# Two cross attentions and two feed-forward blocks on one core: the inverse softmax sums of the second attention spread by DMA instead of a matmul

## The chip, the cores and the metric

The kernel runs on one core of a Trainium2 chip. A core has five engines that run their own instruction streams and wait for each other through semaphores: PE (matrix products into PSUM), DVE and ACT (elementwise work on SBUF and PSUM), POOL (elementwise work, slower) and SP (here only the issuer of DMAs). Sixteen DMA engines move data between DRAM and SBUF. The metric is the device time of one execution in microseconds; of repeated runs the median is taken.

## The reference, cut to what matters

The input x is 8 batches (B) of 112 rows (S) of 512 features (D); a context has 375 tokens per batch. Four blocks follow each other, each added to x:

```
x = x + L0_xattn(layernorm(x), ctx)          # scores, softmax, readout
x = x + L0_ffn(layernorm(x))                 # ternary weights, 1408 hidden
x = x + L1_xattn(layernorm(x), ctx)          # 16 heads of 32, the block of the change
x = x + L1_ffn(layernorm(x))                 # integer weights, 1408 hidden
```

In the third block, for each head, with `Wq, Wk, Wv, Wo` and biases:

```
probs = softmax(clip(q k^T / sqrt(32), -50, 50))      # over 375 tokens
ctx   = probs v                                        # 112 x 32 for each of 16 heads
delta = layernorm(clip(residual_scale, 0, 0.3) * (ctx Wo^T + bo)) * gamma + beta
```

The kernel takes the exponentials without dividing them, sums `e v` and `e` over the tokens on PE, and multiplies the context by the inverse of the sum afterwards. The sum belongs to a head and a row; the context has 32 features for a head. So each inverse has to reach 32 partitions. The change is about that step.

## The kernel before, in words

All work is on one core, with the order of every engine's instructions written by hand in one function per engine; only what the semaphores ask is waited for. The tokens of the context are padded to 384, three chunks of 128 (TC = 3). The 896 rows of x (N) are seven tiles of 128 (TILES = 7) outside the attentions, eight batches of 112 inside.

Up to about 255 us the first attention, the first feed-forward block and the keys and values of the second attention are computed; keys and values are spilled to DRAM and fetched again batch by batch by SP (`kst`, `vst`). From 255 to 353 us the loop over the eight batches `b` of the second attention runs. The 16 heads are four groups `g` of four (G = 4), and m = 4b + g numbers the groups. A head group's context lies on 128 partitions as 4 heads x 32 features, so the context of a batch is `ctxt`, 128 partitions x (4 groups x 112 rows). For each m:

- PE `scores(m)`: 12 matmuls (L1527) into PSUM, run two groups ahead of their use.
- ACT `exps(m)`: three exponentials of 128 x 448 (L1253) into `e[g]`.
- DVE `clip(m)`: a clamp of 128 x 1344 in place (L1946).
- PE `values(b, g)`: `e v` into one PSUM bank (L1544) and `e` times the constant `z_pick` into another (L1548), which puts the sum of head `hh` of group `g` on partition 32 hh + g. In batches 0 to 3 the sums of groups 0 and 1 are first added over the token chunks by POOL (`fold`, L1025 and L1027) and picked at the end of the batch (L1556).

After the fourth group: ACT `sums_copy(b)` copies the undivided context from PSUM to `ctxt` (L1259, counts `u_copied`); DVE `invert(b)` takes the reciprocal of the sums to `rz`, 128 x 112 (L1952, counts `z_inv`); PE `spread(b)` multiplies `rz` with the constant matrix `z_spread`, four fp32 matmuls of 112 columns (L1564, counts `z_ready`), which puts inverse g of head hh on its 32 partitions in the freed sums' bank; DVE `normalize(b)` multiplies `ctxt` by that bank (L1958, counts `ctxt_scaled`); POOL `value_bias(b)` adds the values' bias (L637, counts `ctxt_ready`). The banks for context and sums alternate between (6, 7) and (4, 5) for the first batches (`D_UZ`) and are (4, 5) from batch 3 on, because banks 6 and 7 then serve the output projection; `values(b, 0)` waits until the batch before in the same banks is normalised (`UZ_BEFORE`).

Three batches behind, tile t of the output projection follows: ACT `context_high` and DVE `context_low` split the context into two halves (L653, L686), PE `project(t)` multiplies by the split `wo_p` (L673; the split itself is made in batches 2 and 3 by ACT L1283 and DVE L2001), DVE `delta_variance`, POOL `delta_inverse`, DVE `x3_statistics`, POOL `x3_inverse`, DVE `x3_shift` do the layer norms, ACT `x3_normalized`, PE `normalized_turn` (L681), ACT `turned_high` and DVE `turned_low` give the transposed input `xt` of the last block.

The order inside batch b before the change is: on PE `project(b-4)`, `spread(b-1)`, `normalized_turn(b-5)`, then scores and values of the four groups; on DVE `invert(b-1)`, second clamp, `context_low`, `normalize(b-1)`, `delta_variance`, `turned_low`, third clamp, `x3_statistics`, fourth clamp, `x3_shift`, in batch 3 the split of wo, the next batch's first clamp; on ACT `x3_normalized`, `sums_copy(b-1)`, `context_high`, `turned_high`, four groups of exponentials; on POOL `fold`, `value_bias(b-1)`, `delta_inverse`, `fold`, `x3_inverse`, integer conversion of weights. SP's queue fetches keys, values and weights.

From 353 us on the last block runs: `inner_sums(n)` are the gate and up products of one chunk of 128 hidden features (L1597), with ACT `silu_gate` (L1293) and DVE `inner_hidden` (`hf`, L2012) behind them. The first seven are interleaved with the last tiles of the projection (`project(5)`, `project(6)`), with `x3_turn` (L1606) and the late conversions of weights on ACT (`late_integers`, L1306). The down products (L1647) close the kernel.

## Time and profile before

| | |
|---|---|
| device time, median of 3 runs | 472.7 us (471.65 to 473.21) |
| the profiled execution's own time | 472.69 us |
| its span, first to last instruction | 471.0 us |
| mean granted clock of PE | 0.993 of full speed |
| busy: PE, PE weight loads | 443.2 us, 279.1 us |
| busy: DVE, ACT, POOL | 316.1, 244.7, 111.0 us |
| DMA | 82.7 MB in 59183 packets, nearly all on SP's queue |

A row of the profile gives a line of the code, the engine, the operation, its output and inputs with shapes, and times in us (ns where it says so). Busy time says how long an engine worked, not whether anything depended on it. The chain of waits, followed back from the end, tells what did. A window of the trace gives all engines' busy time in a stretch; PEclk in it is the granted clock as a share of 2.4 GHz. SPq is the queue of DMA instructions of SP; the duration of a row there is the issuing of the DMA, not its transfer, for which the time to landing is given.

### The profile page before, as it was taken

How to read it: one execution, taken by the hardware profiler on the slowest of the kernel's cores; microseconds unless marked ns; L12 is line 12 of the kernel's file. 1: busy time of each engine (PE TensorE's matmuls, PEld its weight loads, DVE VectorE, ACT ScalarE, POOL GpSimd, SP SyncE). 2: the span in 40 equal slices, each digit the busy share in tenths (PEclk: the TensorE clock that was granted, in tenths of full speed). 3: DMA queues.
4: the chain of work that ended last, by engine and by line, in shares of the span. 5: the costliest groups of instructions: out<-in, count | busy, mean ns of one | idle time of the engine just before them, and what ended most of it. 6: DMA issues, size and time to landing. Idle time of an engine off the chain costs nothing.

```text
span 471.0 us, 9958 instructions
## 1 busy us (share of the span) xinstructions
PE 443.2 (94%) x3838; PEld 279.1 (59%) x3847; DVE 316.1 (67%) x573; ACT 244.7 (52%) x370; POOL 111.0 (24%) x126
## 2 busy tenths in 40 slices
PE   8999899999899899999998888899999999999997
PEld 5556565655355345454555667577775565556996
DVE  4995596679867877765755455888867985555111
ACT  4755744764666356464847668477744682221000
POOL 2220400025024000001084364644422251000000
PEclk9999999999999999999999899899999999999999
DMA  8998988934795145333497998766242370000111
GB/s 268 328 376 310 372 292 262 330 93 146 219 295 139 53 109 160 78 91 82 111 306 197 272 316 312 266 214 225 85 135 90 90 221 26 0 0 0 48 51 58
DMA packets 59183, 82.73 MB, mean 176 GB/s; under 512 B 20100, under 2 KB 43652, under 8 KB 57988
## 3 DMA queue, kind: packets, MB, share of 16 engines
q1 hardware_dynamic: 59136, 82.14, 55.2%
q8 instruction: 29, 0.48, 0.4%
q14 instruction: 16, 0.11, 0.1%
q10 hardware_dynamic: 2, 0.01, 0.0%
HBM read 58.76 MB, written 14.42 MB: 155 GB/s over the span
## 4 chain that ended last, share of the span: by engine, by line
PE 68%; DVE 12%; SPq 7%; DMA 4%; issue 4%; ACT 2%; POOL 2%; ACTq 0%; DVEq 0%; POOLq 0%
PE psum L1597 13%; PE psum L208 8%; PE psum L206 8%; PE psum L1647 8%; PE psum L1430 6%; PE psum L673 4%; PE psum L1544 3%; PE psum L1439 3%; PE psum L1497 3%; DMA kst<-k_scratch 2%; SPq L237 2%; PE psum L1373 2%; PE psum L1527 2%; PE psum L1548 2%; DMA w_stage<-in_w 2%
## 5 line engine op out<-in xcount | busy, mean ns | idle before, releaser
L208 PE MATMUL psum<-wv_p,kv_p 128*128 128x512 f16 x288 | 66.1, 379 | 0.5 <-DVE khl L228 0.5
L206 PE MATMUL psum<-kv_p,wk_p 128*128 128x376 f16 x384 | 66.0, 322 | 0.3 <-DVE khl L228 0.3
L1253 ACT ACTIVATE e<-psum,mask_bias 128x448 f32<-128x448 f32 x96 | 53.6, 635 | 20.6 <-PE psum L1527 16.1
L206 PEld LDWEIGHTS psum<-kv_p,wk_p 128*128 128x128 f16 x384 | 37.5, 98 | 24.6 <-issue 0.6
L208 PEld LDWEIGHTS psum<-wv_p,kv_p 128*128 128x128 f16 x288 | 28.0, 98 | 32.8 <-issue 1.0
L1946 DVE TENSOR_SCALAR e<-e 128x1344 f32<-128x1344 f32 x32 | 32.3, 1010 | 11.5 <-ACT e L1253 11.5
L1544 PE MATMUL psum<-e,vst 128*32 128x112 f32 x768 | 34.9, 266 | 3.9 <-issue 3.3
L1597 PE MATMUL psum<-xt,wg_b 128*128 128x448 f16 x176 | 36.9, 352 | 0.3 <-issue 0.3
L1597 PE MATMUL psum<-xt,wu_b 128*128 128x448 f16 x176 | 36.9, 352 | 0.0
L1647 PE MATMUL psum<-h_p,wd_r 128*128 x176 | 36.0, 366 | 0.0
L1647 PEld LDWEIGHTS psum<-h_p,wd_r 128*128 128x128 f32 x176 | 33.1, 188 | 2.7
L355 POOL TENSOR_SCALAR w_stage<-w_stage,w_stat 128x2816 f32<-128x2816 f32 x6 | 17.1, 2851 | 71.9 <-DVE w_stat L350 71.8
L1293 ACT ACTIVATE gated<-psum,gs 128x448 f32<-128x448 f32 x22 | 13.9, 631 | 38.7 <-PE psum L1597 33.5
L1527 PE MATMUL psum<-qst,kst 128*128 128x112 f16 x384 | 24.9, 215 | 3.6 <-issue 3.2
L2012 DVE SCALAR_TENSOR_TENSOR hf<-psum,sgu,gated 128x448 f32<-128x448 f32 x22 | 15.0, 682 | 19.5 <-ACT gated L1293 19.3
L1597 PEld LDWEIGHTS psum<-xt,wu_b 128*128 (+1 forms) x176 | 17.2, 98 | 16.1
L1597 PEld LDWEIGHTS psum<-xt,wg_b 128*128 (+1 forms) x176 | 17.1, 98 | 15.6 <-issue 0.5
L222 ACT ACTIVATE vsp<-psum 128x512 f32<-128x512 f32 x24 | 14.1, 589 | 23.4 <-PE psum L208 23.4
L1527 PEld LDWEIGHTS psum<-qst,kst 128*128 128x128 f16 x384 | 20.2, 98 | 8.9 <-issue 6.2
L218 ACT ACTIVATE khl<-psum,bqk 128x376 f16<-128x376 f32 x32 | 18.1, 568 | 13.8 <-PE psum L206 13.7
L1544 PEld LDWEIGHTS psum<-e,vst 128*32 128x32 f32 x768 | 19.9, 111 | 7.9 <-issue 4.6
L2064 DVE SCALAR_TENSOR_TENSOR res<-psum,sdn,x3t 128x448 f32 x8 | 5.5, 684 | 28.5 <-PE psum L1647 28.5
(197 smaller groups left out, 853.9 us busy)
## 6 DMA issues: line engine op xcount, KB each, us to landing
kst<-k_scratch SPq DMA_DIRECT2D x32, 384.0 KB, 6.3
kv_raw<-in_ctx_feat SPq DMA_DIRECT2D x12, 768.0 KB, 6.3
w_stage<-in_w SPq DMA_DIRECT2D x6, 1408.0 KB, 8.7
cn<-in_ctx_tok SPq DMA_DIRECT2D x8, 768.0 KB, 9.6
k_scratch<-khl SPq DMA_DIRECT2D x128, 48.0 KB, 2.0
v_scratch<-vsp SPq DMA_DIRECT2D x24, 256.0 KB, 2.8
vst<-v_scratch SPq DMA_DIRECT2D x8, 768.0 KB, 4.6
qst<-qhl SPq DMA_DIRECT2D x32, 112.0 KB, 5.2
```

Source lines behind the costliest of these rows:

```text
L206: mm = pe.matmul(psum[:, kv_bank(p), 0:TQ], wk_p[:, u, k, n * P:(n + 1) * P], src[:, v, k, 0:TQ], **ends)
L208: mm = pe.matmul(psum[:, kv_bank(p), :], src[:, u, k, n * P:(n + 1) * P], wv_p[:, v, k, :], **ends)
L218: act.activation(khl[n][:, 0, 0:TQ], psum[:, kv_bank(p), 0:TQ], ACT.Identity, bias=bqk[:, 1, n:n + 1]).then_inc(kv_hi, 1)
L355: pool.tensor_scalar(w_stage[:, w_half_of[half]], w_stage[:, w_half_of[half]], w_stat[:, 4 * n + 2:4 * n + 3], ROUND, ALU.mult, ALU.add).t ...
L673: mm = pe.matmul(psum[:, E_O, :], ctxt_p[t % 2][:, u, k, :], wo_p[:, v, k, :], start=(k, u, v) == (0, 0, 0), stop=(k, u, v) == (KC - 1, *P ...
L1253: act.activation(e[g][:, c, :], psum[:, D_S + (TC * g + c) % 4, 0:4 * S], ACT.Exp, bias=mask_bias[:, b, c:c + 1], scale=1.0 / (WS * QS)).t ...
L1430: mm = pe.matmul(psum[:, B_GU + 2 * ((q + c) % 2) + n, 0:hi - lo], xqt[q][:, k, :], w[:, k, lo:hi], start=k == 0, stop=k == KC - 1)
L1527: mm = pe.matmul(psum[:, D_S + (TC * g + c) % 4, hh * S:(hh + 1) * S], kst[b % 2][:, g, hh, c * P:(c + 1) * P], qst[b // 4][:, hh, g, b % ...
L1544: mm = pe.matmul(psum[32 * hh:32 * hh + 32, D_UZ[b][0], g * S:(g + 1) * S], vst[b % 2][:, c, (4 * g + hh) * HD:(4 * g + hh + 1) * HD], e[g ...
L1597: mm = pe.matmul(psum[:, F_GU + 2 * q + m, 0:HALF], w[:, k, bass.ts(j, P)], xt[:, u, k, a * HALF:(a + 1) * HALF], start=(k, u) == (0, 0), ...
L1647: mm = pe.matmul(psum[:, F_D + m, 0:HALF], wd_r[:, j, m * P:(m + 1) * P], h_p[:, a, u, j, :], start=(j, u) == (0, 0), stop=(j, u) == (JC - ...
L1946: dve.tensor_scalar(e[g][:], e[g][:], EXP_LOW, EXP_HIGH, ALU.max, ALU.min).then_inc(e_ready, 1)
```

## The change

The constant `z_spread` and PE's `spread` go. ACT gets `inverse_store(b)`, a DMA of `rz` (128 x 112 floats) to one of two DRAM buffers `z_scratch`, and `inverse_load(b)`, four DMAs that each read four rows of it (one head's four groups, 448 floats in a row) and write them to the 32 partitions of that head in `zr`. `zr` has four places in SBUF, in regions that are free at the time. In batch b the store of b - 1 is issued after the exponentials m = 4b + 2 and the loads after m = 4b + 4; the store waits for the reciprocal, the loads for the store's landing. `normalize` reads `zr` from SBUF.

Around it: `normalize(b-1)` moves from the second clamp to behind the fourth clamp and `x3_shift`; POOL's `value_bias(b-1)` moves behind both folds, `delta_inverse` and `x3_inverse`; `values` and the last block wait for `u_copied` and `z_inv` in place of `ctxt_scaled`; after the loop the loads of batch 7 stand behind the first silu and `late_integers(4)`, `normalize(7)` behind `x3_statistics(4)`, and `context_high(6)`, `context_low(6)`, `delta_variance(6)` and `project(6)` move back.

```diff
-        z_spread = at("z_spread", [P, G, 4, HD], F32, 190720 + 1024)
...
+        zr = [at(f"zr{q}", [P, G, S], F32, where) for q, where in enumerate((172288, 174080, 36352, 38144))]
...
+            return zr[(2 if b >= 3 else 0) + b % 2]
...
+        z_scratch = nc.dram_tensor("z_scratch", (2, P, S), F32).ap()
...
# project
-            pe.wait_ge(ctxt_scaled, 3)
+            pe.wait_ge(u_copied, 3)
# normalized_turn
+            pe.wait_ge(z_inv, 3)
# POOL, before the loop
-            pool.memset(z_spread[:], 0.0).then_inc(ones_set, 1)
-            pool.wait_ge(ones_set, 3)
+            pool.wait_ge(ones_set, 2)
...
-            pool.affine_select(out=z_spread[:], in_=z_spread[:], compare_op=ALU.not_equal, fill=1.0, base=0,
-                               pattern=[[-1, G], [-HD, 4], [0, HD]], channel_multiplier=1).then_inc(ones_set, 1)
# POOL, the loop
                 if FOLDED[b]:
                     fold(b, 0)
-                if b:
-                    value_bias(pool, b - 1)
                 if b >= 4:
                     delta_inverse(pool, b - 4)
                 if FOLDED[b]:
                     fold(b, 1)
                 if b >= 4:
                     x3_inverse(pool, b - 4)
+                if b:
+                    value_bias(pool, b - 1)
...
+            delta_inverse(pool, 4)
             value_bias(pool, B - 1)
-            for t in range(4, TILES):
+            x3_inverse(pool, 4)
+            for t in range(5, TILES):
# ACT
+            def inverse_store(b):
+                act.wait_ge(z_inv, b + 1)
+                after(act, z_ready, 64 * (b - 1))
+                act.dma_start(z_scratch[b % 2], rz[:]).then_inc(z_stored, 16)
+            def inverse_load(b):
+                act.wait_ge(z_stored, 16 * (b + 1))
+                after(act, ctxt_scaled, b - 1)
+                if b == 3:
+                    act.wait_ge(wo_lo, 1)
+                for hh in range(4):
+                    act.dma_start(zr_of(b)[HD * hh:HD * hh + HD].rearrange("p g s -> p (g s)"),
+                                  z_scratch[b % 2, HD * hh:HD * hh + G].rearrange("(o g) s -> o (g s)", o=1)
+                                  .to_broadcast([HD, G * S])).then_inc(z_ready, 16)
...
                     if m < G * B:
                         exps(m)
+                    if b and g == 0:
+                        inverse_store(b - 1)
+                    if b and g == 2:
+                        inverse_load(b - 1)
...
             sums_copy(B - 1)
+            inverse_store(B - 1)
             context_high(act, 5)
             turned_high(act, 3)
...
             silu_gate(0, 0, 0, 0)
             late_integers(4)
+            inverse_load(B - 1)
             silu_gate(1, 1, 0, 1)
-            context_high(act, 6)
             x3_normalized(act, 4)
             late_integers(5)
             silu_gate(2, 0, 0, 2)
+            context_high(act, 6)
# PE
-                    after(pe, ctxt_scaled, UZ_BEFORE[b] + 1 if UZ_BEFORE[b] is not None else 0)
+                    if UZ_BEFORE[b] is not None:
+                        pe.wait_ge(u_copied, UZ_BEFORE[b] + 1)
+                        pe.wait_ge(z_inv, UZ_BEFORE[b] + 1)
...
-                    spread(b - 1)
...
-                    if g == 0 and 1 <= b < 4:
-                        spread(b - 1)
...
-            spread(B - 1)
...
             x3_turn(1)
+            inner_sums(3, 1, 0, 3)
             project(pe, 6)
-            inner_sums(3, 1, 0, 3)
# DVE
-                after(dve, ctxt_scaled, b)
+                after(dve, z_stored, 16 * b)
                 dve.reciprocal(rz[:], psum[:, D_UZ[b][1], 0:S]).then_inc(z_inv, 1)
...
-                dve.wait_ge(z_ready, b + 1)
+                dve.wait_ge(z_ready, 64 * (b + 1))
                 dve.wait_ge(u_copied, b + 1)
                 u = ctxt[:, :, b * S:(b + 1) * S]
-                dve.tensor_tensor(u, u, psum[:, D_UZ[b][1], 0:G * S].rearrange("p (g s) -> p g s", g=G),
-                                  ALU.mult).then_inc(ctxt_scaled, 1)
+                dve.tensor_tensor(u, u, zr_of(b)[:], ALU.mult).then_inc(ctxt_scaled, 1)
...
-                if b:
-                    normalize(b - 1)
                 if b >= 4:
                     delta_variance(dve, b - 4)
...
                 if b >= 4:
                     x3_shift(dve, b - 4)
+                if b:
+                    normalize(b - 1)
...
             turned_low(dve, 3)
-            normalize(B - 1)
...
             x3_statistics(dve, 4)
+            normalize(B - 1)
             inner_step(1, 1, 0, 1)
-            context_low(dve, 6)
             x3_shift(dve, 4)
             delta_variance(dve, 5)
             inner_step(2, 0, 0, 2)
             x3_statistics(dve, 5)
-            delta_variance(dve, 6)
+            context_low(dve, 6)
             x3_shift(dve, 5)
             inner_step(3, 1, 0, 3)
+            delta_variance(dve, 6)
```

## Rows read from the trace of the kernel before

**Rows 1.** The page, busy time, share of the span and instructions of each engine.

```profile
PE 443.2 (94%) x3838; PEld 279.1 (59%) x3847; DVE 316.1 (67%) x573; ACT 244.7 (52%) x370; POOL 111.0 (24%) x126
```

**Rows 2.** Windows: batch 3, batch 5, project(0); columns in the first line.

```profile
core 0: us, PE busy (x) PEld busy (x) DVE busy (x) ACT busy (x) POOL busy (x), PEclk, DMA share, GB/s
290.40:301.40 11.00, 8.45 (x217) 6.92 (x215) 10.92 (x8) 6.36 (x12) 9.54 (x6) 1.00 0.78 267
314.70:327.00 12.30, 12.15 (x270) 9.59 (x264) 10.46 (x19) 9.33 (x18) 5.16 (x8) 1.00 0.68 236
301.40:305.40 4.00, 4.00 (x16) 1.46 (x13) 2.51 (x4) 2.11 (x5) 1.17 (x2) 0.59 0.69 210
```

**Rows 3.** The chain of waits from 250 to 400 us, shares by line.

```profile
by line: PE psum L1597 19.3%; PE psum L673 12.6%; PE psum L1544 9.9%; DMA kst<-k_scratch 7.1%; PE psum L1527 6.5%; PE psum L1548 6.4%; issue 5.9%; PE psum L1564 3.9%; POOL zs L1027 3.1%; DVE e L1946 2.2%; ACT e L1253 2.2%; POOL zs L1025 1.9
```

**Rows 4.** Lines 1564, 1952, 1958, 1259: duration ns min/median/max, first and last start, forms.

```profile
L1564 PE MATMUL psum<-rz,z_spread x64: 259/275/515, 268.5 to 354.5; 128*128 128x112 f32 x64
...
L1952 DVE RECIPROCAL rz<-psum x8: 839/856/858, 265.4 to 352.7; 128x112 f32<-128x112 f32 x8
...
L1958 DVE TENSOR_TENSOR ctxt<-ctxt,psum x8: 607/620/622, 270.6 to 354.9; 128x448 f32<-128x448 f32 x8
...
L1259 ACT ACTIVATE ctxt<-psum x8: 543/545/551, 265.4 to 352.7; 128x448 f32<-128x448 f32 x8
```

**Rows 5.** The chain of waits in batch 5: start us, us, what.

```profile
314.81 2.70 PE psum L673 x12
317.50 0.89 PE psum L1564 x8
```

**Rows 6.** Timeline of batch 5, scores and exponentials: start us, us, engine, line.

```profile
320.63 0.77 PE L1527 MATMUL psum<-qst,kst 128*128 128x112 f16 x12
...
322.61 0.76 PE L1527 MATMUL psum<-qst,kst 128*128 128x112 f16 x12
...
323.08 1.68 ACT L1253 ACTIVATE e<-psum,mask_bias 128x448 f32<-128x448 f32 x3 [0.30 <-PE psum L1527]
```

**Rows 7.** SP's DMA instructions: issue in ns (min/median/max); landing in us of k_scratch.

```profile
L237 SPq DMA_DIRECT2D k_scratch<-khl x128: 302/427/3856, 25.6 to 232.0; - x128
...
DMA to landing us min/median/max: 1.5/2.0/10.3
...
L263 SPq DMA_DIRECT2D vst<-v_scratch x8: 325/332/597, 254.1 to 327.1; - x8
...
L560 SPq DMA_DIRECT2D qst<-qhl x32: 549/606/1784, 242.6 to 268.9; - x32
```

**Rows 8.** DMA issues, KB each, median us to landing: 262 to 300, 300 to 360 us.

```profile
kst<-k_scratch SPq DMA_DIRECT2D x15, 384.0 KB, 7.8
...
kst<-k_scratch SPq DMA_DIRECT2D x8, 384.0 KB, 5.2
```

**Rows 9.** Timeline of batch 3 and the start of batch 4.

```profile
293.52 3.25 ACT L1253 ACTIVATE e<-psum,mask_bias 128x448 f32<-128x448 f32 x6 [0.54 <-PE psum L1527]
...
294.46 1.48 POOL L637 TENSOR_TENSOR ctxt<-ctxt,bqk 128x448 f32<-128x448 f32 x1 [1.16 <-DVE ctxt L1958]
...
296.58 3.22 DVE L2001 SCALAR_TENSOR_TENSOR wk_p<-wk_raw,wk_p 128x2048 f16<-128x2048 f32 x1
...
300.84 0.59 PE L1556 MATMUL psum<-zs,z_pick 128*32 128x112 f32 x16 [2.29 <-POOL zs L1027]
...
301.37 4.45 PE L673 MATMUL psum<-wk_p,ctxt_p 128*128 128x512 f16 x12
```

**Rows 10.** Timeline of the first steps of the last block.

```profile
360.74 0.71 ACT L1306 ACTIVATE wu_b<-gu_int,zero_point 128x512 bf16<-128x512 int32 x1
...
363.87 0.67 DVE L2012 SCALAR_TENSOR_TENSOR hf<-psum,sgu,gated 128x448 f32<-128x448 f32 x1
...
367.58 2.75 PE L673 MATMUL psum<-wk_p,ctxt_p 128*128 128x512 f16 x12
...
372.49 0.18 DVE L710 BATCH_NORM_AGGREGATE ln_mv<-ln_stat 128x2 f32<-128x6 f32 x1
...
373.20 0.60 PE L681 MATMUL psum<-ident,xn_e 128*128 128x128 f32 x4
```

More of the change, by code:

```diff
@@ L564, in build, with zr_of @@
         rz = at("rz", [P, S], F32, 78080)
+        zr = [at(f"zr{q}", [P, G, S], F32, where) for q, where in enumerate((172288, 174080, 36352, 38144))]
+        def zr_of(b):
+            return zr[(2 if b >= 3 else 0) + b % 2]
+        z_scratch = nc.dram_tensor("z_scratch", (2, P, S), F32).ap()
+        z_stored = sem("z_stored")
         zs = [at(f"zs{g}", [P, 4 * S], F32, where) for g, where in enumerate((194304, 194304 + 1792))]
@@ L1007, in _ @@
             pool.memset(z_pick[:, :, G:HD], 1.0).then_inc(ones_set, 1)
-            pool.memset(z_spread[:], 0.0).then_inc(ones_set, 1)
-            pool.wait_ge(ones_set, 3)
+            pool.wait_ge(ones_set, 2)
             pool.affine_select(out=z_pick[:, :, 0:G], in_=z_pick[:, :, 0:G], compare_op=ALU.not_equal, fill=1.0, base=0,
                                pattern=[[1, G], [-1, G]], channel_multiplier=0).then_inc(ones_set, 1)
-            pool.affine_select(out=z_spread[:], in_=z_spread[:], compare_op=ALU.not_equal, fill=1.0, base=0,
-                               pattern=[[-1, G], [-HD, 4], [0, HD]], channel_multiplier=1).then_inc(ones_set, 1)
-            pool.wait_ge(ones_set, 5)
+            pool.wait_ge(ones_set, 3)
             pool.affine_select(out=z_pick_last[:], in_=z_pick[:], compare_op=ALU.is_ge, fill=0.0, base=T - 1 - 2 * P,
@@ L1537, in values @@
                     if b < 2:
-                        pe.wait_ge(ones_set, 6)
+                        pe.wait_ge(ones_set, 4)
                         pe.wait_ge(q_lo, G + 2 * (b + 1))
-                    after(pe, ctxt_scaled, UZ_BEFORE[b] + 1 if UZ_BEFORE[b] is not None else 0)
+                    if UZ_BEFORE[b] is not None:
+                        pe.wait_ge(u_copied, UZ_BEFORE[b] + 1)
+                        pe.wait_ge(z_inv, UZ_BEFORE[b] + 1)
                 for c in range(TC):
@@ L1558, in values @@
                 mm.then_inc(pv_sum, 1)
-            def spread(b):
-                pe.wait_ge(z_inv, b + 1)
-                for g in range(G):
-                    mm = pe.matmul(psum[:, D_UZ[b][1], g * S:(g + 1) * S], z_spread[:, g].rearrange("p h d -> p (h d)"), rz[:],
-                                   start=True, stop=True)
-                mm.then_inc(z_ready, 1)
             query(1, 0)
@@ L1613, in _ @@
             project(pe, 5)
-            pe.wait_ge(ctxt_scaled, B)
+            pe.wait_ge(u_copied, B)
+            pe.wait_ge(z_inv, B)
             x3_turn(0)
```

## The prediction

> **What bounds the kernel now.** I read the page first: PE is busy 94% of the span and no other engine over 67% [rows 1]. Then the windows, one for each batch of the second attention: in batch 5 PE is busy for 12.15 of 12.30 us, DVE for 10.46 and ACT for 9.33; in batch 3 PE has 8.45 us of work in 11.0 us and DVE has 10.92 [rows 2]. So PE sets the end in the later batches, with DVE 2 us behind it, and in batch 3 something else does. The chain of waits from 250 to 400 us says how much the removed matmuls hold: L1564 has 3.9% of 150 us, 5.9 us, and POOL's two sums of the folded batches 5.0% [rows 3]. That is all that the change can win directly on PE.
>
> **What is removed.** Eight spreads of 8 matmul records each [rows 4]; one takes 0.89 us on the chain in a late batch [rows 5]. POOL's two initialising steps go too; they lie beside PE's queries, where nothing waits for POOL: 0.
>
> **What is added.** For each batch ACT issues one store (128 x 112 floats, 57 KB) and four loads (57 KB each), 40 DMAs. ACT has issued none in this stretch, so their price on its queue is bounded by SP's: the 49 KB spills took 302 ns at least and 427 in the median, the plain loads of vst 332, the query stack 606 [rows 7]. The shapes are plain rows like vst's, so I take 0.33 us: a store 0.33, four loads 1.3. The first issue can lie beside the last exponential's 0.56 us (1.68 for three [rows 6]), so four loads delay ACT by 0.8. Bounds: 0 (all beside exponentials already dispatched) and 4 x 0.606 - 0.5 = 1.9. Landing: the 49 KB spills, also to DRAM, land 1.5 us after issue at least and 2.0 in the median [rows 7]; counted from the end of the issue I take 1.6, bounds 1.2 and 3.0. In the crowded stretch of batches 1 to 3, where kst takes 7.8 us against 5.2 later [rows 8], I scale that by 1.5 to 2.4.
>
> On the landing the Trainium skill speaks against the change: "DMA: Bandwidth & Descriptors", section "Anatomy of one DMA", has a fixed cost of about 2.0 us for each DMA, most of it the wait for the target memory's receipt, DRAM the slowest. The spills' 1.5 us is below it. By that figure, an estimate, the sum below would come about 1 us higher.
>
> SP's queue keeps its DMAs and their order; POOL issues none. On the 16 engines that all share, only the first store (57 KB) runs ahead of the keys of batch 2, the one load that PE waits for; it is a seventh of one 384 KB key load, and I count 0, with 1 us as the other bound.
>
> **What waits now.** The product with the inverse sums is moved behind the fourth clamp of its batch on DVE, and the load is issued by ACT only after the exponentials m = 4b + 4. So DVE, which gets there one group of exponentials earlier, stands until the landing. Queued behind are the next batch's first clamp, its reciprocal and, in batch 3, the split of wo (L2001). ACT's store in turn waits for that reciprocal. I price this in three places.
>
> Batch 3: in the trace ACT ends exponentials 15 and 16 at 293.52 + 3.25 = 296.8 and DVE starts the split of wo at 296.58 [rows 9]. After the change ACT carries six more issues in batches 2 and 3 (2.0 us, of which I hide 0.5 in its gaps): 298.3. Loads 0.8, landing 2.4, product 0.62 [rows 4], split 3.22 [rows 9]: 305.3. Project(0) needs it, and starts now at 301.4 [rows 9]. The cost is +3.9. The gain of the change is inside it: value_bias (1.48 us) no longer stands between POOL's two sums [rows 9], so PE's 2.29 us wait for POOL goes, but wo is late next. Project(0) takes 4.4 us now against 2.70 in batch 5 [rows 5, 9]: after PE's idle time the granted clock is at its lower level, 1.2 GHz, for most of it (0.59 in the window [rows 2], 1.00 in batch 5). It would be so again. 0.
>
> Batches 4 to 7: a loop of two batches. From a landing on, DVE does its whole batch until the fourth clamp, 10.5 us [rows 2] and some 0.5 of handovers: 11.0. Then PE: last values 1.3, project 2.7, transposes 0.6 [rows 10], two groups of scores and values at 1.98 each, the next scores 0.47 until the exponentials start and 1.68 for these [rows 6]: 10.75. Then loads 0.8, landing 1.6. Together 24.15, or 12.1 a batch, against 12.2 now. The 0.89 us that PE saves is thus used up by DVE's wait: -0.1 in each of three periods, -0.3.
>
> The end: the first inner sums need turned_low(3), and ACT's store, waiting for the reciprocal, now stands in front of context_high and turned_high. Context_high starts now behind the copy of the sums (0.55 [rows 4]); after the change behind reciprocal and store, 0.86 + 0.33 and some 0.1 of handovers: 1.3, so +0.8. Then the last loads stand behind ACT's silu and integers, which end at 361.4 [rows 10]: 362.2, landed 363.8, product until 364.4, so that hf of step 1 starts 0.5 later than 363.87 [rows 10]. Context_low(6) is moved behind x3_statistics(5), which ends at 372.67 [rows 10]. With 0.5 added and its own 0.7 moved out and in again it ends at 373.2, and with the 0.8 at 374.0. Project(6), now at 367.58 [rows 10], can only start then. PE has inner sums 3 beforehand and idles from 371.4, 2.6 us. The trace's row for such a gap (2.29 us) is followed by a project at the lower clock [rows 2, 9], so I take 4.4 us, not 2.75: 378.4 against 373.2 [rows 10], +5.2, of which about 1.0 comes back because DVE is then ahead of the later tiles. Cost with the 0.8: +4.2 (bounds +1.2 and +7).
>
> **Sum.** 3.9 - 0.3 + 4.2 = +7.8 us. The profiled execution took 472.69 us (span 471.0 and 1.7 around it), which is the median of the runs shown, 472.7. So 480.5. The other edits (values waiting for u_copied and z_inv in place of ctxt_scaled) cost nothing while the reciprocal comes early; it now sits behind the landing, the product and a clamp (0.62 + 1.0 + 0.84 = 2.5 us after the landing). PE comes to these values 1.3 + 2.7 + 0.6 + 0.7 = 5.3 us after the fourth clamp. So project and transposes cover it while DVE's wait for the landing stays under 2.8 us; each us more would be a us of PE.
>
> **Rivals.**
> ACT's issues are hidden and the landing is short (faster). The place is the four loads after each second pair of exponentials. It decides from the point where load issue and landing together stay under about 1.5 us. With 0 and 1.2 us the loop is (21.75 + 1.2) / 2 = 11.5, close to PE's own 12.2 - 0.9 = 11.3, so batches 4 to 7 gain 4 x 0.9 = 3.6; batch 3 then costs 0.7 (296.3 + 2.0 + 0.62 + 3.22 = 302.1) and the end 1.2: -1.7, 471.0, and down to 468 if project(6) finds cover. For it: ACT is idle for 3 of 12.3 us [rows 2]. Against it: SP's issues are nowhere under 0.3 us [rows 7], and DVE still waits for exponentials that PE produces in order. Chance 0.17.
>
> The Trainium skill is on this rival's side: the same page, section "Issuing engines are not separate DMA queues", calls the issuing time usually small relative to the DMA itself. In the rows 0.33 stands against 1.5 to 2.0, which is not small here, since five stand in one batch.
>
> Both prices at their upper end (much slower): issue 0.606, landing 3.0, because stores and loads run among 384 KB key loads. Batch 3: 299.9 + 1.9 + 3.0 + 0.62 + 3.22 = 308.6, +7.2. Loop (21.75 + 1.9 + 3.0) / 2 = 13.3, +3.4 in three periods. End +6.7. Sum +17.3, 490.0. For it: kst's 7.8 us in these stretches [rows 8]; against it: the spills' median of 2.0. Chance 0.15.
>
> It cancels (no change): the saved 0.89 us a batch pays for a shorter wait in front of wo and a tail that hides project(6); 472.7 within 1.4 us. It needs every wait at about its half. Chance 0.12.
>
> My forecast has 0.56. A measurement of this kernel can tell about 0.3%, 1.4 us. Faster 0.17, same 0.12, slower 0.56 + 0.15 = 0.71. The likeliest case alone reaches from 475 to 487. The range over all is 471 to 488, with half of the fast rival below and two thirds of the slow one above.
>
> **What would show it.** Right: DVE's product waits 2 to 5 us for the DMA in batches 1 to 3 and 0 to 2 us later; ACT shows five issues a batch of about 0.33 us; wo's split starts near 302; project(0) starts 3 to 5 us later than 301.4; batches 4 to 7 keep a period near 12.1; PE idles before project(6). Wrong: issues under 0.1 us or beside the exponentials, DVE not waiting for zr, periods of 11.4, or a split of wo that ends before PE wants it. If the keys of batch 2 land 2 us or more later, the traffic was what I missed.

## The result, and the profile after

The changed kernel takes 497.8 us (median of 4 runs, 496.3 to 498.9) against 473.0 beside it: a ratio of 1.0525 [1.0483, 1.0567], 25 us slower. The direction was right; the size was three times the predicted 7.8 us and lies outside the range of 471 to 488. Two of the traces used below, of POOL's order alone and of the changed last block alone, are of executions in a slower state (478.4 and 480.6 us against medians of 473.7 and 474.4), so they are used only to show which wait and which clock stands where.

The page after: busy time of the engines, and ACT's DMA queue. PE has 3.8 us more on its busy time than in [rows 1] although 64 matmul records are gone, because more of its work ran at the lower clock (mean 0.964 of full speed against 0.993). PE's share fell from 94% to 90%: the loss is waiting.

```profile
PE 447.0 (90%) x3774; PEld 277.7 (56%) x3783; DVE 316.1 (64%) x573; ACT 245.0 (49%) x370; POOL 114.5 (23%) x124
...
q10 hardware_dynamic: 2690, 2.31, 1.8%
```

The lines of the product (L1979), the store (L1273) and the loads (L1282): duration in ns, then what they waited for and how long they took to land. They stand for [rows 4] and [rows 7].

```profile
L1979 DVE TENSOR_TENSOR ctxt<-ctxt,zr x8: 607/626/627, 285.0 to 384.5; 128x448 f32<-128x448 f32 x8
its engine sat idle before it (us, times) until:
  DMA zr<-z_scratch: 32.9, 7
...
L1273 ACTq DMA_DIRECT2D z_scratch<-rz x8: 343/344/391, 269.2 to 371.6; - x8
...
DMA to landing us min/median/max: 1.6/2.0/8.9
...
L1282 ACTq DMA_DIRECT2D zr<-z_scratch x32: 308/445/1347, 278.1 to 380.4; - x32
...
DMA to landing us min/median/max: 1.8/2.9/7.3
```

DVE stood 32.9 us in front of seven products. By batch, issue to landing: the stores of batches 0 to 7 took 8.9, 6.2, 1.6, 3.6, 2.2, 1.6, 1.6, 1.7 us, and the longest of the four loads 5.6, 5.4, 2.9, 3.0, 7.3, 2.7, 4.9, 2.0. The two worst stores are the first two.

The timeline of batches 1 to 4, without the rows between (start us, us, engine, line; in brackets the idle time before it and its releaser):

```profile
269.15 0.39 ACTq L1273 DMA_DIRECT2D z_scratch<-rz  x1
...
275.54 1.69 ACT L1260 ACTIVATE e<-psum,mask_bias 128x448 f32<-128x448 f32 x3 [3.13 <-PE psum L1557]
...
278.08 1.74 ACTq L1282 DMA_DIRECT2D zr<-z_scratch  x4
...
285.01 0.63 DVE L1979 TENSOR_TENSOR ctxt<-ctxt,zr 128x448 f32<-128x448 f32 x1 [11.71 <-DMA zr<-z_scratch]
...
286.32 0.85 DVE L1973 RECIPROCAL rz<-psum 128x112 f32<-128x112 f32 x1
...
286.46 1.35 PE L1576 MATMUL psum<-e,vst 128*32 128x112 f32 x24 [4.75 <-DVE e L1967]
...
287.20 0.35 ACTq L1273 DMA_DIRECT2D z_scratch<-rz  x1
...
290.70 1.69 ACT L1260 ACTIVATE e<-psum,mask_bias 128x448 f32<-128x448 f32 x3 [0.62 <-PE psum L1557]
...
293.44 2.52 ACTq L1282 DMA_DIRECT2D zr<-z_scratch  x4
...
296.08 1.68 ACT L1260 ACTIVATE e<-psum,mask_bias 128x448 f32<-128x448 f32 x3 [3.70 <-issue]
...
300.96 0.63 DVE L1979 TENSOR_TENSOR ctxt<-ctxt,zr 128x448 f32<-128x448 f32 x1 [9.63 <-DMA zr<-z_scratch]
...
302.41 1.35 PE L1576 MATMUL psum<-e,vst 128*32 128x112 f32 x24 [4.75 <-DVE e L1967]
...
303.18 0.63 ACT L660 ACTIVATE ctxt_p<-ctxt 128x512 f16<-128x512 f32 x1 [3.18 <-POOL ctxt L644]
...
308.31 0.64 ACT L1260 ACTIVATE e<-psum,mask_bias 128x448 f32<-128x448 f32 x1
...
311.86 0.62 DVE L1979 TENSOR_TENSOR ctxt<-ctxt,zr 128x448 f32<-128x448 f32 x1 [3.02 <-DMA zr<-z_scratch]
...
312.40 2.29 DVE L2021 SCALAR_TENSOR_TENSOR wk_p<-wk_raw,wk_p 128x2048 f16<-128x2048 f32 x1
...
314.79 5.28 PE L680 MATMUL psum<-wk_p,ctxt_p 128*128 128x512 f16 x12 [3.60 <-issue]
```

Read it as a ring. The store goes at 269.15 and lands at 278.05; ACT, standing on that, issues the loads at 278.08; the last lands at 285.0 and DVE multiplies. Behind the product on DVE's queue are the clamp that PE's values want (PE idle 4.75 us) and the next reciprocal, which the next store wants. So the next round starts 18 us after this one, and the same happens again: store 287.20, loads 293.44, product 300.96, PE idle 4.75 us.

The rows also say which part of the ring is long. ACT ends the exponentials in front of the first loads at 275.54 + 1.69 = 277.23, so the store's 8.9 us delay the loads by only 0.85 us; the four loads themselves, issue and landing, fill 6.9 of DVE's 11.71 us. In the second round it is 1.0 us for the store and 7.5 for the loads, of DVE's 9.63. There ACT sits idle for 3.70 us with exponentials queued behind it: 1.0 of it for the store's landing, 2.5 for issuing the four loads. Later it stands 3.18 us in front of context_high(0) for POOL's value_bias. The split of wo, which I expected near 302, starts at 312.40, and project(0) at 314.79 instead of 301.37 [rows 9].

The windows of batches 1, 2, 3 and 6 (the same columns as [rows 2]):

```profile
266.00:281.50 15.50, 10.83 (x220) 8.92 (x219) 3.68 (x4) 7.15 (x13) 5.69 (x4) 0.78 1.04 307
281.50:294.90 13.40, 8.55 (x205) 7.03 (x201) 5.83 (x6) 5.51 (x11) 7.67 (x5) 0.87 0.82 284
294.90:311.00 16.10, 9.19 (x204) 7.19 (x204) 7.85 (x7) 9.95 (x17) 8.00 (x5) 0.79 0.64 206
...
341.20:357.10 15.90, 12.75 (x264) 9.91 (x256) 10.29 (x18) 8.16 (x16) 5.84 (x6) 0.89 0.48 144
```

The same for batches 1 and 2 in the kernel before:

```profile
265.30:279.00 13.70, 10.22 (x223) 8.67 (x221) 5.10 (x7) 7.31 (x14) 7.03 (x5) 0.88 1.04 293
279.00:290.40 11.40, 8.75 (x220) 7.22 (x218) 5.99 (x7) 8.87 (x15) 6.52 (x5) 1.00 0.94 373
```

In batch 1 after the change DVE worked 3.7 of 15.5 us; the 16 DMA engines were full, as they were before (share 1.04 in both). The granted clock is 0.78 to 0.89 here, after PE's idle stretches, where it was 0.88 in batch 1 and 1.00 in batches 2 and 3. The keys take as long as in [rows 8] (median landings 7.7 and 4.8 us).

Four late rows of PE: the values of batch 6, the first two products of the inner sums, project(6).

```profile
347.76 0.55 PE L1576 MATMUL psum<-e,vst 128*32 128x112 f32 x8 [2.69 <-DVE rz L1973]
...
373.96 2.00 PE L1617 MATMUL psum<-xt,wg_b 128*128 128x448 f16 x8 [2.76 <-issue]
...
375.76 3.08 PE L1617 MATMUL psum<-xt,wu_b 128*128 128x448 f16 x8
...
394.56 4.27 PE L680 MATMUL psum<-wk_p,ctxt_p 128*128 128x512 f16 x12 [3.18 <-DVE ctxt_p L694]
```

And the rows of the kernel before at the first inner sums:

```profile
353.59 1.15 PE L1564 MATMUL psum<-rz,z_spread 128*128 128x112 f32 x8 [0.40 <-DVE rz L1952]
355.05 1.67 PE L1597 MATMUL psum<-xt,wg_b 128*128 128x448 f16 x8 [0.31 <-issue]
```

Where the 25 us are, by the starts of project(t) and of the down product in the two traces:

| stretch | before | after | more |
|---|---|---|---|
| until project(0) | 301.4 | 314.8 | 13.4 |
| project(0) to project(3) | 37.7 | 42.3 | 4.6 |
| project(3) to project(5) | 22.0 | 24.6 | 2.6 |
| project(5) to the down product | 70.5 | 75.0 | 4.5 |

### The profile page after: what moved, and what is told of

It reads as the page before. It is cut to its first block, busy times and chain, and to the rows that moved or that the text cites. A ratio compares the mean times of both kernels' runs of the same rounds, so it can differ in the third digit from the quotient of the medians.

```text
span 496.0 us, 9886 instructions
## 1 busy us (share of the span) xinstructions
PE 447.0 (90%) x3774; PEld 277.7 (56%) x3783; DVE 316.1 (64%) x573; ACT 245.0 (49%) x370; POOL 114.5 (23%) x124
## 4 chain that ended last, share of the span: by engine, by line
PE 61%; DVE 10%; issue 8%; SPq 7%; DMA 4%; ACT 4%; POOL 4%; ACTq 1%; DVEq 0%; POOLq 0%
PE psum L1617 13%; PE psum L208 8%; PE psum L206 7%; PE psum L1668 7%; PE psum L1460 5%; PE psum L680 3%; PE psum L1469 3%; PE psum L1527 3%; DMA zr<-z_scratch 2%; PE psum L1576 2%; PE psum L1403 2%; ACT e L1260 2%; SPq L237 2%; DMA w_stage<-in_w 2%; PE psum L1557 2%
## 5 line engine op out<-in xcount | busy, mean ns | idle before, releaser
L1576 PE MATMUL psum<-e,vst 128*32 128x112 f32 x768 | 38.2, 292 | 16.4 <-DVE e L1967 13.7
L1617 PE MATMUL psum<-xt,wu_b 128*128 128x448 f16 x176 | 38.3, 362 | 0.0
L1557 PE MATMUL psum<-qst,kst 128*128 128x112 f16 x384 | 28.8, 229 | 7.1 <-DMA kst<-k_scratch 2.4
L1576 PEld LDWEIGHTS psum<-e,vst 128*32 128x32 f32 x768 | 22.0, 121 | 20.6 <-DVE e L1967 17.7
L1557 PEld LDWEIGHTS psum<-qst,kst 128*128 128x128 f16 x384 | 22.7, 106 | 15.0 <-issue 7.0
L680 PE MATMUL psum<-wk_p,ctxt_p 128*128 128x512 f16 x84 | 23.4, 437 | 6.8 <-issue 3.6
L1979 DVE TENSOR_TENSOR ctxt<-ctxt,zr 128x448 f32<-128x448 f32 x8 | 5.0, 623 | 32.9 <-DMA zr<-z_scratch 32.9
```

The costliest lines, as they stand in the source:

```text
L680: mm = pe.matmul(psum[:, E_O, :], ctxt_p[t % 2][:, u, k, :], wo_p[:, v, k, :], start=(k, u, v) == (0, 0, 0), stop=(k, u, v) == (KC - 1, *P ...
L1557: mm = pe.matmul(psum[:, D_S + (TC * g + c) % 4, hh * S:(hh + 1) * S], kst[b % 2][:, g, hh, c * P:(c + 1) * P], qst[b // 4][:, hh, g, b % ...
L1576: mm = pe.matmul(psum[32 * hh:32 * hh + 32, D_UZ[b][0], g * S:(g + 1) * S], vst[b % 2][:, c, (4 * g + hh) * HD:(4 * g + hh + 1) * HD], e[g ...
L1617: mm = pe.matmul(psum[:, F_GU + 2 * q + m, 0:HALF], w[:, k, bass.ts(j, P)], xt[:, u, k, a * HALF:(a + 1) * HALF], start=(k, u) == (0, 0), ...
```

## Experiments

Ratios are against the kernel before, run beside them; times in us. Milestones of the runs, from their timelines. Each is one execution: the two runs with hops in batches 3 to 5, whose code is that of before until then, have project(0) 1.3 and 1.7 us later than before, so differences of that size between two rows say little:

| kernel | project(0) | (3) | (5) | (6) | down product | ratio to before |
|---|---|---|---|---|---|---|
| before | 301.4 | 339.1 | 361.1 | 367.6 | 431.6 | |
| after | 314.8 | 357.1 | 381.7 | 394.6 | 456.7 | 1.0525 [1.048, 1.057] |
| no hops | 301.3 | 334.7 | 357.5 | 370.3 | 432.4 | 0.9983 [0.993, 1.003] |
| no hops, old tail | 301.0 | 334.3 | 355.4 | 361.9 | 425.9 | 0.9907 [0.986, 0.995] |
| late product | 305.6 | 343.3 | 369.3 | 382.1 | 444.0 | 1.0302 [1.023, 1.037] |
| slack | 303.4 | 340.2 | 364.4 | 371.6 | 436.1 | 1.0153 [1.010, 1.021] |
| hops in 3 to 5 | 303.1 | 338.1 | 362.1 | 368.6 | 432.6 | 1.0013 [0.998, 1.005] |
| the same, early low part | 302.7 | 337.8 | 359.9 | 366.4 | 430.4 | 0.9938 [0.991, 0.997] |

**No hops.** The changed kernel without stores, loads and their waits; the product is an in-place maximum, so the inverse sums are not applied.

```diff
-                    if b and g == 0:
-                        inverse_store(b - 1)
-                    if b and g == 2:
-                        inverse_load(b - 1)
...
-                dve.wait_ge(z_ready, 64 * (b + 1))
-                dve.tensor_tensor(u, u, zr_of(b)[:], ALU.mult).then_inc(ctxt_scaled, 1)
+                dve.tensor_tensor(u, u, u, ALU.max).then_inc(ctxt_scaled, 1)
```

> The changed kernel without store and loads: normalize takes the larger of the context and itself, so the context of the second attention stays undivided. Theory A (the waits for the two landings make the loss): everything of the 24.8 us goes and PE's removed spreads show, so 460 to 470 us against 473. Theory B (the new places of the steps make it, tail and value_bias above all): it stays at 480 or above. If the waits are the cause, the idle time of DVE in front of L1979 (32.9 us now) is near zero and project(0) starts before 301 us.

Measured 0.9983, 473.2 us: the whole loss is the hops', as theory A has it. But the gain that I had expected with it, 460 to 470 us, is missing; where it went is shown further below, at the order of the last block. Project(0), project(3) and project(6) in its timeline:

```profile
301.34 2.75 PE L680 MATMUL psum<-wk_p,ctxt_p 128*128 128x512 f16 x12 [0.78 <-issue]
...
334.71 2.76 PE L680 MATMUL psum<-wk_p,ctxt_p 128*128 128x512 f16 x12
...
370.30 4.45 PE L680 MATMUL psum<-wk_p,ctxt_p 128*128 128x512 f16 x12 [3.16 <-DVE ctxt_p L694]
```

Project(0) starts when it did before, yet takes 2.75 us and not 4.45 [rows 9]: PE's wait of 2.29 us in front of it is now one of 0.78, and the clock stays up. From there to project(3) it takes 33.4 us against 37.7: 1.7 is that, the rest (2.6) is what three spreads of 0.89 cost. The 4.4 us are lost again before the down product.

**Hops that nobody waits for.** As no hops, but with all 40 DMAs on ACT's queue in their shapes (constants stored, rows of wo loaded into a place that nobody reads).

```diff
-                act.dma_start(z_scratch[b % 2], rz[:]).then_inc(z_stored, 16)
+                act.dma_start(z_scratch[b], ones_f[:, 0:S]).then_inc(z_stored, 16)
```

> The 40 DMAs stay at their places on ACT's queue with the same shapes and sizes, but read constant data and write a place that nobody reads, and nothing waits for their landing; the context stays undivided. It tells the issue and the traffic from the waits. Theory A (landings): within 2 us of the run without hops. Rival C (issue on ACT's queue and load on the 16 DMA engines): more than 8 us above it, most of the 24.8 us kept, with ACT idle before the exponentials for the issue of four DMAs (2 to 3 us each batch, issues up to 1.3 us).

Measured 1.0031 [0.999, 1.007]: 0.5% over no hops, and their intervals overlap. Issuing and traffic together are some 2 of the 25 us, and by the ends of the intervals at most 6; the rest is waiting. The landings of its stores, and what SP issued around the first one (at 268.4, landed 9.0 us later):

```profile
DMA to landing us min/median/max: 1.6/3.8/9.0
...
262.69 5.71 SPq L559 DMA_DIRECT2D qst<-qhl  x8
268.45 0.59 SPq L263 DMA_DIRECT2D vst<-v_scratch  x1
269.09 2.48 SPq L258 DMA_DIRECT2D kst<-k_scratch  x4
```

So the long landings don't come from the waits: a 57 KB store issued among query, value and key loads takes as long as these (kst 9.2 in the median of this stretch).

**Late product.** The product of batch b behind the reciprocal of the next batch, so that these are no longer queued behind the landing; POOL's value_bias moves with it.

```diff
                 if b:
                     invert(b - 1)
+                if b >= 2:
+                    normalize(b - 2)
```

> The changed kernel with the product of batch b-1 moved on DVE from in front of the next batch's first clamp to behind that batch's reciprocal, and value_bias with it to the start of POOL's next batch. Hops and waits stay, results too. Theory A1 (the loss comes from what is queued behind DVE's wait: clamp, reciprocal, split of wo): 478 to 486 us, DVE's idle time for zr below 10 us. Theory A2 (ACT's wait for the store's landing, 8.9 and 6.2 us in batches 1 and 2, makes it): 490 or more, with ACT idle in front of exponentials 9 and 13 as now.

DVE's wait for `zr` fell from 32.9 to 3.2 us, yet the time only from 1.0525 to 1.0302 (486.9 us, just above the 478 to 486 of theory A1). By the milestones 9.2 us came back until project(0) and 4.6 until project(3), the whole loss of that stretch; behind it nothing did, and 1.2 more were lost. ACT still stands 9.4 us for POOL's value_bias in front of context_high (13.7 in the changed kernel), which still stands ahead of the exponentials, and the last block keeps its whole loss. Moving one wait is not enough.

**POOL's order alone.** The kernel before with value_bias behind both folds.

> The kernel before with one edit of the change alone: value_bias(b-1) behind both folds on POOL in the batches that fold. The prediction said that this takes PE's 2.29 us wait for POOL in front of project(0) away, and with it the slow clock of project(0): 469.5 to 471.5 us, 1.5 to 3 us faster. Rival: context_high and the split of wo are next, no change within 1 us.

1.0035 [1.000, 1.007]: no gain, as the rival said. In its trace the wait for POOL is gone and project(0) takes 2.76 us, but PE idles 1.14 us for the split of wo, and in the next batch 2.23 us with the lower clock behind it. PE's wait in front of project(0) was real; that edit by itself is worth nothing that can be measured.

**Slack.** Every part gets a batch more: loads behind the last exponentials, product in the middle of the next batch, context_high and context_low behind it, the last block as before.

```diff
-                    if b and g == 2:
-                        inverse_load(b - 1)
+                    if b >= 3 and g == 2:
+                        context_high(act, b - 3)
+                    if b and g == 3:
+                        inverse_load(b - 1)
...
                 clip(G * b + 2)
+                if b >= 2:
+                    normalize(b - 2)
...
                     x3_shift(dve, b - 4)
-                if b:
-                    normalize(b - 1)
+                if b >= 3:
+                    context_low(dve, b - 3)
```

> The hops keep their DMAs, but every wait gets most of a batch: loads of batch b-1 behind the last exponentials of batch b, product and value_bias in the middle of batch b+1, context_high and context_low behind the third and fourth group, the order after the loop as in the kernel before, the last loads in front of the first silu. Theory A (the loss is only what stands behind waits for the landings): DVE and ACT wait under 5 us in all, period of batches 4 to 7 near the 11.1 us of the run without hops, 467 to 471 us, below the kernel before. Rival (landings of 5 to 9 us still reach the reciprocal or the exponentials in batches 1 to 3): 474 to 480.

1.0153, 478.9 us: 18 of the 25 us are back, not all; it is the rival's 474 to 480. The product's idle time, the store's landings, and two late projects:

```profile
  DMA zr<-z_scratch: 6.1, 3
...
DMA to landing us min/median/max: 1.6/5.4/8.5
...
340.20 2.76 PE L680 MATMUL psum<-wk_p,ctxt_p 128*128 128x512 f16 x12 [0.57 <-DVE ctxt_p L694]
352.23 2.76 PE L680 MATMUL psum<-wk_p,ctxt_p 128*128 128x512 f16 x12 [3.82 <-DVE ctxt_p L694]
```

In the first batches a store of 8 us and a load of 5 are longer than a batch of 11 to 12, so some landing is late in this order too; and with context_low last on DVE, PE waits for DVE in place of the spread. My expectation had both too small.

**Small key loads.** In both kernels the key loads from batch 2 on bring 24 KB in place of 384 KB, so these batches' scores are computed from stale keys; instruction counts stay.

```diff
-                         .to_broadcast([2 * HD, 2, 4 * TP])).then_inc(kst_loaded[b % 2], 16)
+                         .to_broadcast([2 * HD, 2, cols])).then_inc(kst_loaded[b % 2], 16)
```

> The changed kernel, but each key load from batch 2 on moves 24 KB instead of 384 KB (the rest of the keys is stale). Theory L (SP's key loads make the landings long): stores land in about 1.6 us and loads in 2.0 to 2.5 us in batches 1 to 3 too, and the kernel gains 8 to 14 us, to 484 to 490. Rival (the hops are slow in themselves, or PE and DVE set the pace): landings stay above 4 us there, gain under 4 us.

> The kernel before with the same small key loads. It holds no hop, so it gains only its one wait for keys: 2 to 3 us, 470 us. The difference to the run of the changed kernel with small keys is the price of the hops at short landings: 13 to 17 us by theory L; 24 if the key loads do not matter.

1.0269 [1.020, 1.034] for the changed kernel, 0.9939 [0.990, 0.998] for the one before: the hops then cost 3.3%, 15.6 us (by the intervals 12 to 20), in place of 25. In that run of the changed kernel, the product's idle time and the loads' landings:

```profile
  DMA zr<-z_scratch: 17.4, 7
...
DMA to landing us min/median/max: 1.8/2.1/5.1
```

The loads land in 2.1 us in place of 2.9 in the median, and DVE's waiting nearly halves. So some 9 of the 25 us are landings made long by the key traffic. The path is not idle in this run: the first three stores still took 5.7, 4.8 and 2.4 us, where I had expected 1.6, since query and value loads are as before. The milestones of the two runs with small keys, 299.5, 335.3, 357.3 and 427.8 before and 308.1, 344.2, 367.8 and 442.5 after the change (project(0), (3), (5), down product), say where the rest is: 8.6 us until project(0), 0.3 until project(3), 1.6 until project(5) and 4.2 in the last block. With shorter landings the loop of batches 4 to 7 costs nearly nothing; batches 1 to 3 and the last block still do.

**Keys one by one.** SP waits for the landing of each key load before it issues the next.

```diff
                     keys_fetch(sp, b + 2, g)
+                    sp.wait_ge(kst_loaded[b % 2], 16 * (G * (b // 2 + 1) + g + 1))
```

> The changed kernel, but SP waits for the landing of each key load from batch 2 on before it issues the next, so that at most one 384 KB load is queued; bytes are the same. If ACT's DMAs stand behind what SP has queued before them, stores and loads of batches 2 and 3 land in 2 to 4 us instead of 5.4 to 6.2 (the store of batch 0 stays long, behind values and query stack). If they only share the bandwidth, landings stay where they are. The kernel's time is not the point: 485 to 500.

One execution: 525.4 us, where I had expected 485 to 500. Its stores' landings, and kst's in the stretch from 262 to 300 us:

```profile
DMA to landing us min/median/max: 1.6/1.6/3.4
...
kst<-k_scratch SPq DMA_DIRECT2D x7, 384.0 KB, 3.5
```

With SP's queue kept short no store takes over 3.4 us (8.9 in the changed kernel), and a key load takes 3.5 and not 7.7. PE waits 27 us for keys and DVE 61 for `zr`; the loss against the changed kernel is 27.6. The loads of `zr` did not get shorter: their median went from 2.9 to 4.7 us. The run does not tell order from shared bandwidth, though: the wait also pushed the eight query loads, which used to be issued just ahead of the first store, to 11 us behind it, and the DMA traffic between 262 and 300 us fell from 284 to 146 GB/s. It shows that stores land sooner with less of SP's in flight; by which of the two stays open, for the loads as well.

**The order of the last block.** First without hops (and so without applying the inverse sums), with the last block in the order of before, the product of batch 7 included; then the kernel before with the changed order.

```diff
             x3_turn(1)
-            inner_sums(3, 1, 0, 3)
             project(pe, 6)
+            inner_sums(3, 1, 0, 3)
```

> The changed kernel without stores and loads (the product is an in-place maximum, so the inverse sums are not applied), and its last block back in the order of the kernel before. The run without hops reached project(3) 4.4 us earlier than the kernel before and came out level with it. If the order of the last block is what gave those 4.4 us back, project(6) here starts near 363 and the run takes 468 to 469. If the last block absorbs the 4.4 us whatever its order (because the integers, the residuals or the late tiles are due at fixed times there), it takes 472 to 473.

> The kernel before, with nothing but its last block in the changed kernel's order: context_high(6) behind the third silu, context_low(6) behind x3_statistics(5), delta_variance(6) behind inner step 3, inner sums 3 ahead of project(6). If that order costs what the run without hops suggests, project(6) starts 4 to 5 us later at the lower clock and the run takes 476 to 477. If it costs nothing by itself, 473.

0.9907 and 1.0025 [0.999, 1.006]. Project(6) of the first:

```profile
361.88 2.75 PE L680 MATMUL psum<-wk_p,ctxt_p 128*128 128x512 f16 x12
```

Back in the old order, project(6) comes 6.5 us after project(5) at full clock, in place of 12.8 and 4.45 us at the lower one; the ratios differ by 0.76%, 3.6 us, with 3 us of noise on it. Put into the kernel before, the same order of project(6) costs 1.2 us, not clear of nothing, and at most 2.9, where I had expected 3 to 4: there the product of batch 7 stays where it was, PE waits 1.93 us for context_low(6), and project(6) then takes 2.76 us. So the price is not in the order alone: it needs the longer gap (3.16 us without hops) and the clock that was lower after it.

**Hops in batches 3 to 5 alone.** The kernel before; batches 0 to 2, 6 and 7 keep the spread, 3 to 5 take the hops with their product a batch later.

```diff
+        HOPPED = (3, 4, 5)
...
+                if b - 2 in HOPPED:
+                    normalize(b - 2)
+                if b and b - 1 not in HOPPED:
+                    normalize(b - 1)
```

> The kernel before; only batches 3, 4 and 5 take the hops, with their products one batch later, and the others keep the spread on PE; last block as before. Theory (the price is in landings behind key loads and in who waits for them): stores of 3 to 5 land within 5 to 6 us of issue, so the load can go out behind the third pair of exponentials, and lands 2 to 3 us later, about when DVE comes to the product: PE keeps up to 3 x 0.9 us, 470 to 472. Rival (two hops do not fit beside these batches wherever they are put, since DVE and ACT have no idle time left for them): DVE waits over 1 us in each of three batches for zr or for the later context_high, and the run takes 474 or more.

1.0013, 473.5 us: level, where I had expected 470 to 472. No product waited for a DMA, and from project(0) to project(3) the three spreads were saved (35.0 us against 37.7). Then:

```profile
338.06 2.76 PE L678 MATMUL psum<-wk_p,ctxt_p 128*128 128x512 f16 x12
349.52 2.76 PE L678 MATMUL psum<-wk_p,ctxt_p 128*128 128x512 f16 x12 [1.85 <-DVE ctxt_p L691]
```

Project(4) waits 1.85 us for context_low(4), which now comes after the product of a batch earlier, value_bias and context_high. A last run moved these two in batch 7 only.

```diff
                 clip(G * b + 2)
+                if b == B - 1:
+                    context_low(dve, b - 3)
```

> As the run with hops in batches 3 to 5 alone, but in batch 7 context_high(4) goes one group of exponentials earlier and context_low(4) ahead of x3_statistics(3) on DVE. In the trace of that run project(0) to project(3) took 35.0 us against 37.7 before, that is the three spreads, and project(4) then waited 1.85 us for context_low(4), which gave 2.0 of it back. With the theory that this order alone is what gave it back, project(4) waits under 0.5 us, project(6) comes 2 to 2.7 us earlier relative to project(0) than before, and the run takes 470 to 471. If the time is given back later still (x3_statistics(3) late, the tail waiting for it), it takes 473.

```profile
337.84 2.76 PE L678 MATMUL psum<-wk_p,ctxt_p 128*128 128x512 f16 x12
347.37 2.76 PE L678 MATMUL psum<-wk_p,ctxt_p 128*128 128x512 f16 x12
```

The wait is gone, project(4) follows project(3) after 9.5 us, and the time is 470.7 us, as expected, against 472.6 beside it, 0.9938 [0.991, 0.997]: 0.6% faster than the kernel before, small but clear of the noise. One product waited 1.2 us for its loads. Three hops pay a little, where their landings have cover and PE is the bound.

## Why the prediction failed, point by point

- **What PE can win** (0.89 us a batch): right. Without hops and with the old last block the gain is 0.9%, 4.4 us (2 to 6 by the interval).
- **Issue price** (0.33 us; bounds 0 to 0.6): the store's 0.344 fits. A load took 0.445 in the median, and the third or fourth of a row up to 1.35, above my bound. It mattered little: in batch 3 they ran beside exponentials; in batch 2 the four kept ACT from its exponentials for 2.5 us, for which I had 0.8; all unwaited hops together cost about 0.5%.
- **The step that failed, batch 3 (+3.9; measured +13.4).** It is the first term, "298.3", the end of exponentials 15 and 16: batches 1 and 2 had no wait in my sum, only six issues. They have the same ring of store, load, product, clamp and reciprocal. There DVE stood 11.7 and 9.6 us and PE 4.75 us each time, and the exponentials ended at 308.31 + 0.64 = 308.95, 10.7 us later than in my sum. The terms behind it held: from there to project(0) I had 7.0 us and the trace has 5.8, with a landing of 2.9 where I had 2.4 and the split of wo shorter (2.29 against 3.22). What made the two rounds so long is the landing, where I scaled by 1.5 to 2.4 us: the loads took 5.6 and 5.4, the stores 8.9 and 6.2. kst's own 7.8 us stood in [rows 8], and the small DMAs were nearly as slow as that. But with small key loads, where the landings of the loads are about as I had them, 8.6 us are still lost until project(0). So the missing rounds are the step, and the landing is the size. ACT's own wait on the store's landing had no term either; it is 0.9 and 1.0 us.
- **Batches 4 to 7** (-0.3; measured +4.6, all until project(3)): 0.9 of it is the second period and 3.8 the third, 15.9 us between project(2) and project(3) where it was 12.1. There the loads landed after 7.3 us, not 1.6; DVE waited 4.63 for them and PE 2.69 behind the reciprocal. That roughly fits the condition that beyond 2.8 us of DVE's wait each us more would be a us of PE (1.8 us by it). The loop itself was right in kind: with small key loads it costs 0.3 us. (Its PE terms add up to 10.71, not 10.75.) Project(0) took 5.28 us where it took 4.45, since PE had idled 3.60.
- **The end** (+4.2; measured +7.1, all that comes after project(3)): right in kind, small in size. The first inner sums waited 2.76 us, where the rows before have 0.40, a spread of 1.15 and 0.31: 0.9 more, for which I had 0.8. Then their first two products ran at the lower clock, 2.00 and 3.08 us where they took 1.67 and 1.68; these 1.7 us I did not have. Project(6) waited 3.18 and took 4.27 us, near my 2.6 and 4.4; the 1.0 that I let come back afterwards hardly did, for its wait and its extra 1.5 us are 4.7, and 4.5 are lost from project(5) to the down product. With small key loads the last block loses the same 4.2: it is not the landing's size.
- **value_bias**: the wait for POOL went, and wo was late next, as predicted. Without hops project(0) took 2.75 us in place of 4.45, for which I had 0; but POOL's order alone, with the same short project(0), gave no gain in time, so no worth of it is shown.
- **Traffic**: PE could start on the keys of batch 2 at 275.05 us against 273.46, 1.6 later, of which 0.65 stem from before the first store. That is under the 2 us that I had named as a sign.
- **Rivals.** The slow one (490.0) was the nearest, with 308.6 for project(0) where 314.8 came: it too had no wait in the first two batches, and its 3.0 us for a landing was too short for them. The cancelling and the fast one needed short waits everywhere and fell with them.

On the landing, the Trainium skill ("DMA: Bandwidth & Descriptors", "Anatomy of one DMA") has a fixed 2.0 us, in a section on DMAs that GpSimd issues; the hops are ACT's. The fastest stores here took 1.6 and loads 1.8, a little under it; the 8.9 is far above it. The same page's "Queues, rings and completion order" lets each DMA engine serve the rows of queues in turn, a packet at a time. From that one could expect that a small store on ACT's row does not stand behind all that SP has queued. The first store does not meet that expectation: 9.0 us, where kst takes 9.2, with nobody waiting for it. No run here shows in which order the engines served the two rows, so the page's rule itself is not tested.

## What to carry to other kernels

In the crowded batches of this kernel a small DMA took nearly as long as the large ones in flight beside it, so price it by the landings of its neighbours at the moment it is issued, not by the same DMA elsewhere. Where a wait for it stands on an in-order queue, follow the ring: who is queued behind the wait, and whether the next DMA's source is among them; then a late landing can be paid once a batch from the first batch on, and also in batches that seem to have slack. To move small work from PE to DMA, do it only in the stages that PE bounds, with a stage of slack, and look for the next late operand (here context_low), which can give the whole gain back.

## What the runs showed that I had not expected

- A 57 KB store took 8.9 us, and 9.0 with nobody waiting; 3.3 when SP kept one key load in flight and the eight query loads came behind it. Even so the 8.9 us delayed the loads by only 0.85, because ACT had exponentials to do meanwhile.
- Of four DMAs issued in a row by ACT (at 307.6 us), the first two took 0.31 and 0.5 us and the last two together 1.8.
- Project(0) takes 2.75 us after an idle of 0.78 us, 4.45 after one of 2.29, and 5.28 after one of 3.60 after the change; 4.70 after one of 5.14 with keys one by one.
